# Masked 16-head attention: maxima limited before the subtraction, in place of marks added to the reciprocals

## What is computed

```python
def _L2_xattn_ref(q, k, v, mask, Wq, bq, Wk, bk, Wv, bv, Wo, bo):
    B, S, D, H = (2, 256, 128, 16)
    DH = D // H
    ...
    scores = jnp.einsum('bhqd,bhkd->bhqk', qh, kh) / math.sqrt(DH)
    scores = jnp.where(mask, -jnp.inf, scores)
    attn = jax.nn.softmax(scores, axis=-1)
    out = jnp.einsum('bhqk,bhkd->bhqd', attn, vh)
    out = out.transpose(0, 2, 1, 3).reshape(b, -1, D)
    return out @ Wo + bo
```

## Time and profile before

| | |
|---|---|
| median of 3 runs | 516.43 us (516.41 to 518.99) |
| the profiled execution | 515.07 us, span 513.2 us |
| busy: PE, DVE, ACT, POOL | 440.6, 353.3, 257.6, 138.2 us |
| instructions: PE, DVE, ACT, POOL | 2726, 771, 486, 210 |
| mean granted TensorE clock | 0.95 of full speed |

### The profile page before, as it was taken

The page is one execution under the profiler, slowest core; times in us unless marked ns, Lnnn a source line. Parts: engine busy times, 40 slices in busy tenths (PEclk is TensorE's granted clock), DMA queues, the critical chain, the costliest instruction groups (busy, mean ns, idle before and its releaser), DMA issues.

```text
span 513.2 us, 8106 instructions
## 1 busy us (share of the span) xinstructions
PE 440.6 (86%) x2726; PEld 345.4 (67%) x2726; DVE 353.3 (69%) x771; ACT 257.6 (50%) x486; POOL 138.2 (27%) x210
## 2 busy tenths in 40 slices
PE   7989999999999998999998879889628899976095
PEld 4778989999999997889996446665214677532044
DVE  5658787777877876563357867965776765457984
ACT  3667767777577765344422325553441466215811
POOL 4520041321300002021007347574223543000000
PEclk9999999999999999699999999999958999989579
DMA  7799000000000000000000000000000000000001
GB/s 219 224 151 67 5 1 2 0 0 0 0 0 0 1 1 0 1 1 1 1 0 1 0 1 1 1 2 0 1 1 0 0 1 1 1 1 0 0 0 42
DMA packets 28456, 9.38 MB, mean 18 GB/s; under 512 B 17918, under 2 KB 27915, under 8 KB 28427
## 3 DMA queue, kind: packets, MB, share of 16 engines
q1 hardware_dynamic: 27164, 8.38, 10.0%
q10 hardware_dynamic: 1263, 0.61, 0.4%
HBM read 8.47 MB, written 0.52 MB: 18 GB/s over the span
## 4 chain that ended last, share of the span: by engine, by line
PE 63%; DVE 21%; issue 5%; ACT 4%; POOL 4%; DMA 1%; ACTq 1%; POOLq 0%; DVEq 0%
PE bank L835 6%; PE bank L464 6%; PE bank L466 5%; PE bank L465 5%; PE bank L975 5%; PE bank L824 4%; PE bank L825 4%; PE bank L1085 4%; PE bank L459 3%; PE bank L856 3%; PE bank L1264 2%; DVE inv L1944 2%; POOL scratch L679 2%; DVE stats L1599 2%; PE bank L1099 2%
## 5 line engine op out<-in xcount | busy, mean ns | idle before, releaser
L1674 DVE TENSOR_TENSOR probT_lo<-bank,probT_hi 128x512 fp32r<-128x512 f32 (+1 forms) x80 | 55.1, 688 | 23.7 <-ACT probT_hi L1352 23.6
L1352 ACT ACTIVATE probT_hi<-bank 128x512 fp32r<-128x512 f32 (+1 forms) x80 | 47.5, 594 | 42.7 <-PE bank L835 42.7
L1667 DVE TENSOR_REDUCE neg_max<-bank 128x1 f32<-128x589 f32 x64 | 49.2, 768 | 17.8 <-PE bank L825 16.8
L459 PE MATMUL bank<-ones 128*128 128x512 f32 x108 | 56.5, 656 | 1.8 <-POOL ident L529 1.8
L1343 ACT ACTIVATE shared<-bank,neg_max 128x589 f32<-128x589 f32 x64 | 48.0, 749 | 4.9 <-DVE neg_max L1667 4.9
L835 PE MATMUL bank<-ident,shared 128*128 128x128 f32 (+1 forms) x320 | 48.0, 272 | 0.4 <-ACT shared L1343 0.4
L679 POOL TENSOR_TENSOR scratch<-scratch,neg_max 128x1232 f32<-128x1232 f32 x16 | 36.0, 2248 | 35.0 <-DVE neg_max L1930 35.0
L600 POOL TENSOR_TENSOR rstd<-var_eps,minus_half 128x4 f32<-128x4 f32 x14 | 14.7, 1050 | 113.2 <-DVE var_eps L1605 113.2
L835 PEld LDWEIGHTS bank<-ident,shared 128*128 128x128 f32 (+1 forms) x320 | 39.8, 142 | 2.7 <-ACT shared L1343 0.6
L1085 PE MATMUL bank<-k_blocks,queries 128*128 128x308 f32 x128 | 36.4, 427 | 5.9 <-DVE scratch L1922 2.2
L459 PEld LDWEIGHTS bank<-ones 128*128 128x128 f32 x108 | 21.4, 214 | 20.9 <-issue 19.0
(11 more groups left out here) (349 smaller groups left out, 1108.6 us busy)
## 6 DMA issues: line engine op xcount, KB each, us to landing
shared<-in_mask_Bx16xSxS_bk SPq DMA_DIRECT2D x8, 154.0 KB, 7.7
shared<-in_L_xattn_Wkv SPq DMA_DIRECT2D x8, 128.0 KB, 3.8
w<-in_L_ffn_W SPq DMA_DIRECT2D x1, 1024.0 KB
shared<-in_L_xattn_Wq SPq DMA_DIRECT2D x4, 128.0 KB, 3.6
x_residual<-in_x ACTq DMA_DIRECT2D x2, 256.0 KB, 5.1
shared<-in_L_xattn_Wo SPq DMA_DIRECT2D x4, 128.0 KB, 4.6
out_x<-x_residual SPq DMA_DIRECT2D x1, 512.0 KB, 3.2
wn<-in_L_ffn_w_gate SPq DMA_DIRECT2D x1, 192.0 KB, 3.5
```

The lines of the kernel that those rows point to most:

```text
L459: nc.tensor.matmul(bank[:, at, :].rearrange("p (n m) -> p n m", n=4), ones[:], ones[:].unsqueeze(1).to_broadcast([P, 4, P]), start=True, s ...
L1352: nc.scalar.activation(probT[HI][0:n, SLOT[c], :], bank[0:n, PT_BANK[b][c], :], ACT.Copy)\
L1667: nc.vector.tensor_reduce(neg_max[:, b, i:i + 1], scores0(i), AX.X, ALU.max, negate=True)\
L1674: nc.vector.tensor_tensor(probT[LO][0:n, SLOT[c], :], bank[0:n, PT_BANK[b][c], :], probT[HI][0:n, SLOT[c], :].bitcast(F32), ALU.subtract). ...
```

## The change

The marks go, with their buffers and semaphore: the four GpSimd instructions behind each subtraction, VectorE's addition to the reciprocals, and VectorE's waits for marks. In their place GpSimd limits the negated maxima of a masked tile to 1e37, in place, ahead of the subtraction. In a head with all keys masked every score is about -3e38; less a maximum so limited it stays hugely negative, the exponentials and their sum are 0, the reciprocal is infinite and the product 0 times infinity, NaN. For n = 1 nothing changes.

```diff
             def less_maximum(t, n):
 
                 pool.wait_ge(max16_ok, NT * n + t + 1)
+                if n == 0:
+
+                    own.add(nc.gpsimd.tensor_scalar(neg_max16[:, t % 2, :], neg_max16[:, t % 2, :], 1e37, None, ALU.min))
+                    own.settle()
                 nc.gpsimd.tensor_tensor(s16[:, t % 2], s16[:, t % 2],
                                         neg_max16[:, t % 2, :].unsqueeze(2).to_broadcast([P, HM, NC]), ALU.add)\
                     .then_inc(s16_ok, 1)
...
             for t in range(NT):
                 less_maximum(t, 0)
-                spoil = spoil16[:, t % 4, :]
-                if t:
-                    pool.wait_ge(spoil16_ok, t)
-                if t >= 4:
-                    pool.wait_ge(o16_ok, t - 3)
-                own.add(nc.gpsimd.tensor_scalar(keep16[:], neg_max16[:, t % 2, :], 1e37, None, ALU.is_lt))
-                own.settle()
-                own.add(nc.gpsimd.tensor_scalar(spoil, keep16[:], -1.0, 3e38, ALU.add, ALU.mult))
-                own.settle()
-                own.add(nc.gpsimd.tensor_scalar(spoil, spoil, 3e38, None, ALU.mult))
-                own.settle()
-                nc.gpsimd.tensor_tensor(spoil, spoil, keep16[:], ALU.mult).then_inc(spoil16_ok, 1)
             spread_kv(1)
             inverse_root(5)
...
                         dve.wait_ge(s16_taken, m + 1)
-                        if m >= 2 and n == 0:
-                            dve.wait_ge(spoil16_ok, m - 1)
                         nc.vector.tensor_reduce(neg_max16[:, z, :], s16[:, z], AX.X, ALU.max, negate=True)\
                             .then_inc(max16_ok, 1)
...
                         own.settle()
-                        if n == 0:
-                            dve.wait_ge(spoil16_ok, d + 1)
-                            own.add(nc.vector.tensor_tensor(inv16[:, y, :], inv16[:, y, :], spoil16[:, d % 4, :],
-                                                            ALU.add))
-                            own.settle()
                         each = inv16[:, y, :].rearrange("p (c h) -> p c h", h=2).unsqueeze(3)
                         nc.vector.tensor_tensor(o16[:, t - LAG, :].rearrange("p (c h d) -> p c h d", c=NPAIR, h=2),
```

More of the change, by code:

```diff
@@ L209, in build @@
         neg_max16 = sb("neg_max16", [P, 2, HM])
-        keep16 = sb("keep16", [P, HM])
-        spoil16 = sb("spoil16", [P, 4, HM])
         inv16 = sb("inv16", [P, 2, HM])
@@ L367, in build @@
         max16_ok = sem("max16_ok")
-        spoil16_ok = sem("spoil16_ok")
         p16_ok = sem("p16_ok")
```

## The result

The changed kernel takes 512.95 us (median of 20 runs) and the kernel before 516.21 (20 runs, timed beside it). One of the 20 runs of the changed kernel was slow, 750.88 us at a mean granted clock of 0.55, and the ratio is worked out without it. The ratio is 0.9938 with a 95% interval of 0.9913 to 0.9964, that is 3.2 us less, with 1.9 to 4.5 in the interval. The profiled execution took 515.15 with a span of 513.3; the one of before had 515.07 and 513.2. Of these two executions alone one would say that nothing was gained, and the first thing to learn here is why not.

The account below looks back on a forecast made before the run. The prediction took VectorE's marked additions, waiting for GpSimd's subtraction and paid by TensorE, to bound the masked attention. Marks removed (-3.10) and three limits (+0.99) gave -2.11 us: 516.43 to 514.3 us, range 512.2 to 516.2.

Parts of the forecast that it names:

- The marked addition is a wait for the subtraction: Masked attention: VectorE's addition of marks to reciprocals, both inputs in SBUF, takes 2 us waiting for GpSimd's long subtraction.
- For any tile whose subtraction is in flight: Masked attention: the addition is held in every tile where GpSimd's 2.25 us subtraction is still running.
- Marks removed, -3.10, by the second attention as yardstick: Without marks the masked attention, 53.50 us, should match the unmasked second one, 50.40 us: 3.10 us gained.
- GpSimd's four instructions and VectorE's waits are worth nothing: Masked loop: removing GpSimd's mark work, 1.18 us a tile, gains nothing; VectorE's waits lie within the 3.10.
- A limit delays the subtraction by 0.33: Masked loop on GpSimd: each limit and its handover put the subtraction back 0.33 us, judged from a similar scalar operation.
- Three passages, +0.99: Masked attention: the critical chain passes the limit three times at 0.33 us, costing 0.99 us (0.66 to 1.32).
- Sum -2.11: Whole kernel: marks removed, -3.10, plus limits, +0.99, gives 2.11 us less, a median of 514.3 us.
- the free limit: Rival, masked loop: the limit is covered by later work and costs nothing, giving 513.3 us; chance 13%.
- the inherited stall: Rival, masked attention: VectorE's product takes over the addition's wait, so limits are paid without gain, 517.4 us; chance 5%.
- the held limit: Rival, masked loop: the limit is itself held by VectorE, 1.98 us in three passages, giving 520.3 us; chance 4%.
- the clock's low stretch near 456: TensorE's clock falls near 456 us, costing 1.4 us on the critical path; the sum took it to move along unchanged.
- the rival with the shorter low stretch: Rival, TensorE near 456 us: the low clock stretch shortens or goes, up to 1.4 us more gained, 512.9 us; chance 18%.

Follow-up runs that it names:

- e3: The kernel before, marks kept, with the limit added ahead of GpSimd's subtraction; masked attention 51.89 us against 53.50.
- e5: As e3, marks and limit both kept, but VectorE takes the reciprocals twice, so the marked addition begins later; masked attention 55.47 us against 51.89 in e3.
- e4: The kernel before, marks kept, no limit, but marks added to the sums in PSUM ahead of the reciprocals; masked attention 50.38 us, ratio to before 0.9953.
- e1: The changed kernel without the limit, so without marks or limit; masked attention 50.38 us against 51.39.
- e2: The changed kernel with the limit done twice in a row; masked attention 52.36 us against 51.39.
- e8: The kernel of e1 (changed kernel without the limit), code unchanged, now timed; ratio to before 0.9923, masked attention 50.39 us.
- e9: The kernel of e2 (changed kernel with the limit twice), code unchanged, now timed; ratio to before 0.9994, masked attention 52.36 us.

## Why the prediction was right

- *The marked addition is a wait for the subtraction:* right (e3, e5, the first tile of e4). *For any tile whose subtraction is in flight:* right, but the prediction took it for settled that the subtraction is first. In four of the five held tiles it was first by 0.24 to 0.30 us only, and e3 shows that this lead made most of the cost: without it the stage lost 1.61, though a limit was added. *In the last tiles no subtraction is left, hence 0.18:* true of those tiles, but in e3 the spreading held an addition there for 1.03.
- *Marks removed, -3.10, by the second attention as yardstick:* 53.50 to 50.38 without marks and limit (e1), -3.12.
- *GpSimd's four instructions and VectorE's waits are worth nothing:* e4 keeps them and has 50.38 as well.
- *A limit delays the subtraction by 0.33:* 323.78 to 324.11, 0.33. *Three passages, +0.99:* +1.01 (e1), and +0.97 for a second one (e2); the chain of the changed kernel shows the pair three times, and the begins of the subtractions in e2 agree. (The upper bound of 3.1 counts three passages at 1.04; with the four held possible it would be 4.2. Neither the range nor a chance uses it.)
- *Sum -2.11:* the stage lost 2.11 in each of three profiles, two tiles of the loop take 9.83 where "about 9.8" was named, and the second attention is unchanged.
- *The rivals:* the free limit, the inherited stall and the held limit are ruled out by e1, the product of 0.29 and the limit of 0.25. The sum took the clock's low stretch near 456 to move with the work unchanged. It did not: against the one profile of before it is shorter in two profiles and longer in one.
- *The profiled execution:* a span of 511.1 and a time of 513.0 were named; 513.3 and 515.15 came out. Outside the masked stage the span changed by 2.2 (513.3 - 51.39 = 461.9 against 513.2 - 53.50 = 459.7), more than the half microsecond that the prediction named as a sign of being wrong by the clock. The sum holds for the stage, not for a single execution.
- *The time:* 512.95 lies within 512.2 to 516.2 and 1.4 under the 514.3 named. It lies outside the forecast's own range (513.8 to 514.9), at the 512.9 of the rival with the shorter low stretch; that the median came out where it did is not something the sum foresaw. Of the 1.4, 0.2 is the reference (516.43 was the median of three runs, 516.21 that of twenty). The rest, about 1.1, lies outside the masked stage. By the ratio the change is faster by 0.62% (0.36 to 0.87): the middle lies beyond the 0.5% to which the prediction gave 0.33 (against 0.64 for the same), and the interval leaves both open. The shorter low stretch, 0.5 to 0.7 where it occurred, would explain about half; that it does so in the median is argued from three profiles and not shown, since the timed runs carry no timeline. This stays open.

What I would do otherwise: the two halves of the change don't add up as a sum of parts. Marks first, the removal gives 3.12 and the limit takes 1.01. Limit first, it gives 1.61 (e3) and the removal another 0.50.

No version beat the changed kernel measurably: e4's has a masked attention 1.0 us shorter, and its two ratios (0.9953, 0.9967) are no lower. That of e8 is lower (0.9923), within the noise, but it leaves out the handling of wholly masked heads.

## What to carry to other kernels

If a tiny VectorE instruction takes microseconds, look at what GpSimd does in those microseconds: with two inputs in SBUF it can wait out a whole GpSimd instruction (here 2.04 us beside one of 2.25), and one input in PSUM, or a start a little earlier, frees it. Use a stage of the same program that lacks the suspect as a yardstick, since the sum of the stalls (about 10 us here) says little of what their removal gives (3.1). And measure a gain of half a percent by the stage it falls in: the stage repeated to 0.01 us, 19 of the changed kernel's 20 runs spread over 6.

## What I had not expected of the hardware

An instruction added to GpSimd made the kernel's stage 1.61 us shorter (e3), and one of 0.26 added to VectorE made it 3.58 longer (e5), both by changing which of two instructions began first, by 0.11 and 0.19 us in the tiles shown.

The first part of the program, with the same code, took 300.18 to 305.07 us in twelve profiles; in the two compared above, 1.00 of the 1.28 us between them lies where TensorE's clock stood at 1.2 GHz in one and at 2.4 in the other. And where it stood low behind the masked attention went with the length of that attention: it fell some 10 us behind it in both profiles with 52.36 us and in the one with 51.89, and there in none of the three with 51.39 or the four with 50.38 or 50.39. The place in the span alone doesn't decide it: e8's masked attention ended at 352.59, between those of e2 (352.74) and e9 (352.54), without that fall. These are few profiles, and what makes the difference is not shown.
